# Attention weights turned by VectorE and SBUF-to-SBUF transfers in place of TensorE transposes

## What is computed

```
x: (16, 64, 512)   ctx: (16, 1601, 512)   mask: (64, 1601)   16 heads of 32
q = layernorm(x) @ w_q.T ; k = ctx @ w_k.T ; v = ctx @ w_v.T          (per head)
scores = where(mask == 0, -1e9, q k^T / sqrt(32)) ; attn = softmax(scores)
x = x + (attn v) @ w_o.T
x = x + attention_with_lora(layernorm(x)) ; x = x + experts(layernorm(x))
```

## Time and profile before

| | us |
|---|---|
| time, median of 3 runs | 772.93 (771.41 to 774.77) |
| span of the profiled execution | 772.6 |
| TensorE matmul busy | 708.0 (92%) |
| VectorE busy | 410.2 (53%) |
| ScalarE busy | 360.6 (47%) |
| GpSimd busy | 289.0 (37%) |
| mean granted TensorE clock | 0.960 |
| first value product of batch 0, from the span's start | 59.17 |
| last output product of the cross-attention ends | 471.1 |

### The profile page before, as it was taken

One profiled execution on the slowest core, in us unless ns is written; L12 is line 12 of the kernel. 1 busy time (PEld: TensorE's weight loads), 2 busy tenths in 40 slices (PEclk: granted clock), 3 DMA queues, 4 the chain that ended last, 5 costly groups with the idle time before them and its releaser, 6 DMA issues.

```text
span 772.6 us, 16928 instructions
## 1 busy us (share of the span) xinstructions
PE 708.0 (92%) x6817; PEld 581.6 (75%) x6817; DVE 410.2 (53%) x938; ACT 360.6 (47%) x665; POOL 289.0 (37%) x259
## 2 busy tenths in 40 slices
PE   1999999999999999999999999999999766999970
PEld 0787788778878887888788977887778554788860
DVE  5834434453344424533543345735368348799965
ACT  2425445453545345535454343533455431599950
POOL 0005135513553255225532453432225132788530
PEclk9999999999999999999999999999999985799995
DMA  8401101220021101110110002021001580999818
GB/s 294 149 1 43 45 2 45 98 91 24 29 98 44 44 2 44 44 39 7 44 44 2 3 3 75 1 79 45 3 29 57 188 303 21 330 394 397 333 52 326
DMA packets 30268, 74.77 MB, mean 97 GB/s; under 512 B 4053, under 2 KB 4437, under 8 KB 29155
## 3 DMA queue, kind: packets, MB, share of 16 engines
q1 hardware_dynamic: 25778, 65.16, 23.6%
q0 software_dynamic: 4400, 8.41, 2.9%
HBM read 66.13 MB, written 13.44 MB: 103 GB/s over the span
## 4 chain that ended last, share of the span: by engine, by line
PE 86%; DVE 6%; DMA 3%; ACT 2%; issue 2%; SPq 0%; POOL 0%; DVEq 0%; POOLq 0%; ACTq 0%
PE bank L188 22%; PE bank L190 21%; PE bank L189 20%; PE bank L194 10%; PE bank L345 4%; PE bank L322 3%; DMA raw<-in_wq 2%; DVE x_sb L1611 1%; PE bank L564 1%; DMA wr<-scratch_ys 1%; PE bank L551 1%; PE bank L665 1%; PE bank L580 1%; DVE wh L1084 1%; DVE stats L1340 0%
## 5 line engine op out<-in xcount | busy, mean ns | idle before, releaser
L1637 POOL TENSOR_SCALAR pp<-pp,rl 128x400 f32<-128x400 f32 x128 | 163.8, 1297 | 234.8 <-DVE rl L1162 234.8
L1217 DVE COPY pt<-bank 128x512 f32<-128x512 f32 x64 | 44.3, 692 | 99.4 <-PE bank L194 99.3
L188 PE MATMUL bank<-chi,wk 128*128 128x400 f32 x256 | 93.5, 365 | 0.0
L844 ACT ACTIVATE pp<-pp,acc 128x400 f32<-128x400 f32 x128 | 79.0, 619 | 28.0 <-DVE acc L1250 27.7
L1250 DVE CUSTOM_DVE_ANT_0 pp<-bank,cap 128x400 f32<-128x400 f32 x128 | 66.8, 569 | 46.5 <-PE bank L322 46.5
L190 PE MATMUL bank<-chi,wk 128*128 128x400 f32 x256 | 88.3, 345 | 0.0
L189 PE MATMUL bank<-clo,wk 128*128 128x400 f32 x256 | 88.3, 345 | 0.0
L188 PE MATMUL bank<-wv,chi 128*128 128x512 f32 x200 | 83.5, 417 | 0.0
L189 PE MATMUL bank<-wv,chi 128*128 128x512 f32 x200 | 78.5, 393 | 0.0
L190 PE MATMUL bank<-wv,clo 128*128 128x512 f32 x200 | 78.5, 392 | 0.0
L761 ACT ACTIVATE pt<-bank 128x512 f32<-128x512 f32 x64 | 38.2, 597 | 76.4 <-PE bank L194 75.3
(11 more groups left out here) (238 smaller groups left out, 1387.4 us busy)
## 6 DMA issues: line engine op xcount, KB each, us to landing
wr<-in_We SPq DMA_DIRECT2D x13, 1024.0 KB, 11.6
craw<-in_ctx SPq DMA_DIRECT2D x16, 800.0 KB, 4.4
raw<-in_We SPq DMA_DIRECT2D x8, 1024.0 KB, 10.5
acc<-in_We SPq DMA_DIRECT2D x6, 1024.0 KB, 11.0
scratch_xn<-acc SPq DMA_DIRECT2D x16, 256.0 KB
wr<-scratch_ys SPq DMA_DIRECT2D x8, 512.0 KB, 7.2
x_sb<-in_x SPq DMA_DIRECT2D x2, 1024.0 KB, 8.5
out_dram<-x_sb SPq DMA_DIRECT2D x8, 256.0 KB, 5.9
```

The lines of the kernel that those rows point to most:

```text
L188: pe.matmul(o, lhs[0], rhs[0], start=start, stop=False)
L844: act.activation(frame(p8), frame(p8), ACT.Exp, bias=bias, scale=-1.0, accum_out=total).then_inc(S["a_exp"], 1)
L1217: dve.tensor_copy(pt[:, p8 % 4, :, :].rearrange("p a c -> p (a c)"), at("t", 8 * (n - 1) + p8)[:, :]).then_inc(S["v_pt"], 1)
L1637: pool.tensor_scalar(frame(p8), frame(p8), rl[:, n % 2, p8:p8 + 1], None, ALU.mult).then_inc(S["g_pn"], 1)
```

## The change

- The 32 TensorE transposes of a batch and the 8 copies of their banks go. VectorE now turns each finished frame in blocks of 32x32 (`turn`, one `transpose` of 128x512 per frame) into `square`, which is the space of `raw` read as 16 groups of 256 values per partition.
- SyncE puts the blocks in their place (`shuffle`): for a whole batch 16 transfers from 32 partitions to 32 partitions, in runs of 256 values (1 KB), 128 KB each, from `square` to `pt`. They wait for all eight frames of the batch and for both `pv_part` of the batch before. `pt` is twice as large.
- TensorE's order: keys 0 to 2, first half of the scores, keys 3, the first value tile, both `pv_part` of batch n-1 behind all 16 transfers of it, second half of the scores, the other value tiles. Products of weights and values go to bank 3 (`turned`), so banks 0 to 2 go round.
- VectorE's order: three of the last batch's turnings at the head of a batch, the others behind maxima and shares. ScalarE's exponentials of frames 6 and 7 stand behind the copy of the second value tile.
- `raw` being used, `wo` is loaded and split at batch 0, `w2q` is loaded behind the last transfers, `w2k` behind the barrier to the next stage. `oh` has room for two output tiles, so the third and fourth are filled behind batch 15.

```diff
-        oh = [sb(f"oh{j}", [128, 4, EARLY * 128], f32r, lasting) for j in range(2)]
+        oh = [sb(f"oh{j}", [128, 4, 2 * 128], f32r, lasting) for j in range(2)]
-        pt = sb("pt", [128, 4, 4, 128], f32, second)
+        pt = sb("pt", [128, 4, 4, 256], f32, second)
+        square = raw[:, :].rearrange("p j k n -> p (j k n)").rearrange("p (b x) -> p b x", b=16)
...
+        for n in range(16 * NC_):
+            uses += [("k", 4 * n + g) for g in range(4) if n] + [("v", j) for j in range(made(n), made(n + 1))]
...
         def at(what, i):
-            return pb[use_of[what, i] % 4]
+            return pb[use_of[what, i] % 3]
...
-            def t_part(n, p8):
-                pe.wait_ge(S["g_pn"], 8 * n + p8 + 1)
...
-                turn4(pe, at("t", 8 * n + p8), lambda i4: weight_columns(n, p8, i4)).then_inc(S["p_t"], 1)
             def pv_part(n, half):
-                pe.wait_ge(S["v_pt"], 4 * n + 2 * half + 2)
-                pe.wait_ge(S["a_pt"], 4 * n + 2 * half + 2)
                 if half == 0:
+                    pe.wait_ge(S["d_sh"], 256 * (n + 1))
...
+                for n in range(16 * seg, 16 * seg + NB):
+                    if n:
+                        for g in range(3):
+                            k_part(n, g)
+                    s_part(n, 0)
+                    if n:
+                        k_part(n, 3)
+                    v_part(n, values[0])
+                    if old:
+                        pv_part(n - 1, 0)
+                        pv_part(n - 1, 1)
+                    s_part(n, 1)
+                    for j in values[1:]:
+                        v_part(n, j)
+                for half in range(2):
+                    if not seg:
+                        early_out(2 * half)
+                        early_out(2 * half + 1)
+                    pv_part(last, half)
...
+                    exps(n, seg, 0)
+                    exps(n, seg, 1)
+                    value(n, values[0])
+                    exps(n, seg, 2)
+                    value(n, values[1])
+                    exps(n, seg, 3)
...
+            def turn(n, p8):
+                dve.wait_ge(S["g_pn"], 8 * n + p8 + 1)
+                if n and p8 == 0:
+                    dve.wait_ge(S["d_sh"], 256 * n)
+                c = D * p8 + PW - CW * (n % 8) % 128
+                dve.transpose(square[:, :, 32 * p8:32 * p8 + 32],
+                              pp[:, c:c + 512].rearrange("p (b x) -> p b x", b=16)).then_inc(S["v_pt"], 1)
...
+            def shuffle(n):
+                sp.wait_ge(S["v_pt"], 8 * n + 8)
+                if n:
+                    sp.wait_ge(S["p_pv"], 2 * n)
+                of = square.rearrange("p (i a) x -> p a i x", a=4)
+                for a in range(4):
+                    for to in range(4):
+                        sp.dma_start(pt[32 * to:32 * to + 32, :, a, :],
+                                     of[32 * a:32 * a + 32, to]).then_inc(S["d_sh"], 16)
```

More of the change, by code:

```diff
@@ L229, in perceiver @@
         uses = [("q", m) for m in range(4)] + [("k", g) for g in range(4)] + [("q", 4 + m) for m in range(4)]
[L230 to L241, removed]
+        for n in range(16 * NC_):
+            uses += [("k", 4 * n + g) for g in range(4) if n] + [("v", j) for j in range(made(n), made(n + 1))]
+            if n == NB - 1:
+                uses += [("e", i) for i in range(EARLY)]
         use_of = {use: n for n, use in enumerate(uses)}
         def read_by(what, i):
-            if what == "t":
-                return S["a_pt" if i % 2 else "v_pt"], i // 2 + 1
             if what == "k":
@@ L415, in tensor @@
+                if seg:
+                    spread(last)
             turn_x(0)
@@ L850, in cross @@
-                    value(made(n) + 2)
-                    value(made(n) + 3)
-                    if not seg and 0 <= n - SPLIT < EARLY:
+                    exps(n, seg, 0)
[4 more added lines that the diff above has]
+                    exps(n, seg, 3)
+                    for j in values[2:]:
+                        value(n, j)
+                    if not seg and 0 <= n - SPLIT < 2:
@@ new lines, in cross @@
+                for n in range(first, last + 1):
+                    old = n > first
+                    if old:
+                        for p8 in (5, 6, 7):
+                            turn(n - 1, p8)
+                    if n < last:
+                        context(n + 1)
+                    if n:
+                        k_part(n, 1)
+                    if n == 0:
+                        weight_lo(wh[0], raw[:, 0], 4)
+                    maxima(n, seg, 0)
+                    maxima(n, seg, 1)
+                    share(n, 0, seg)
+                    if n:
+                        k_part(n, 3)
+                    share(n, 1, seg)
+                    turn(n, 0)
+                    turn(n, 1)
@@ L1227, in cross @@
                     if old and seg:
[L1228 removed]
+                        o_more(n - 1, n - 1 - first)
                     elif old:
                         o_first(n - 1)
[L1231 to L1237 removed]
@@ L1261, in cross @@
-                    share(n, 3, seg)
+                    maxima(n, seg, 2)
+                    maxima(n, seg, 3)
+                    share(n, 2, seg)
+                    turn(n, 2)
+                    share(n, 3, seg)
+                    turn(n, 3)
+                    turn(n, 4)
+                    if not seg and 0 <= n - 1 - SPLIT < 2:
+                        dve.wait_ge(S["a_h"], n - SPLIT)
+                        early_lo(n - 1 - SPLIT).then_inc(S["v_h"], 1)
+                for p8 in (5, 6, 7):
+                    turn(last, p8)
@@ new lines, in cross @@
+                if not seg:
+                    for i in range(2):
+                        dve.wait_ge(S["a_h"], i + 3)
+                        early_lo(i + 2).then_inc(S["v_h"], 1)
+                        dve.wait_ge(S["p_o"], i + 1)
+                        early_add(i).then_inc(S["v_x1"], 1)
+                    for i in range(2, EARLY):
+                        dve.wait_ge(S["p_o"], i + 1)
+                        early_add(i).then_inc(S["v_x1"], 1)
+                if seg:
+                    o_more(last, NB - 1)
+                else:
+                    o_first(last)
```

235 lines of the change are left out of this document (87 added, 148 removed).

## The result

The changed kernel takes 781.29 us (median of 5 runs, 777.41 to 783.79), the kernel before on the same chip 772.97 us (771.41 to 775.19): a ratio of 1.0091, 95% interval 1.0057 to 1.0125. It is slower by 0.9%, where 753 us had been forecast. The profiled execution took 777.41 us, its span is 775.6 us, 3.0 above the span before.

The account below looks back on a forecast made before the run. TensorE was taken to bound the batches. Start at 71.6 plus intervals of 347.8 gave 419.4, the end 451.4 in place of 471.1; 19.7 off the 772.6 span, plus 0.3 for the median, gave 753 us, range 728 to 798.

Parts of the forecast that it names:

- What goes: TensorE's transposes, 3.6 us a batch, 58 us in all; intervals would be 21.5 us with three value tiles, 24.4 with four.
- The turnings: VectorE's eight 128x512 transposes a batch, taken at 0.6 us each, 4.8 a batch; the last ends 9.3 behind the second scores.
- rival of longer turnings: VectorE's turnings take twice the length, adding 1.1 us to each of 15 intervals: 770 us, chance 0.05.
- S: Time from first issue to last landing of a batch's 16 transfers, taken as 11.5 us, range 8.5 to 13.2.
- issue-bound: Rival: issuing, not bytes, limits the 16 transfers, 6.2 + 2.3 = 8.5 us to the last landing: 731 us, chance 0.17.
- the circle: Second scores, exponentials, shares, turnings, transfers, `pv_part`, next second scores: 11.5 us plus the transfers' 11.5, 23.0 a batch.
- half-rate rival: Transfers between 32 partitions run at 192 GB/s, 13.2 us to the last landing, intervals of 24.7: 777 us, chance 0.13.
- The clock: TensorE's clock stays up through 1.5 us waits in batches; longer waits at start and end cost 3.3 us each.
- clock rival: TensorE's clock falls at each of thirteen batch waits, 3.3 us each, surely from 2 to 3 us on: 796 us, chance 0.15.
- Start: Splitting `wo` in batch 0 delays second scores from 62.9 to 68.3, a 5.4 us wait, plus 3.3 for the clock: 71.6.
- End: After the last second scores: 20.9 us until transfers land, TensorE waiting 9, then clock 3.3, `pv_part` 2.1, output products 5.7.
- The sum: Start 71.6, fifteen intervals 347.8, then the end to 451.4 in place of 471.1: 19.7 us less, span 752.9.

Follow-up runs that it names:

- e8: Changed kernel with the product of batch n-1 behind second scores and two value tiles, exponentials ahead of value copies, maxima ahead of turnings: 737.4 us, ratio 0.954.
- e4: Changed kernel with eight of each batch's 16 transfers issued by ScalarE and eight by SyncE: 783.8 us, ratio 1.010.
- e11: e10 with all four early output products ahead of the last batch's two products, in place of two ahead and two between: 728.5 us, ratio 0.942.
- e7: Changed kernel with the splitting of `wo` behind the exponentials and maxima of frames 0 to 3 of batch 0: 784.8 us, ratio 1.015.
- e10: e8 with the splitting of `wo` behind the first exponentials and all maxima of batch 0 ahead of VectorE's part: 734.5 us, ratio 0.950.

## Why the prediction was wrong, point by point

- **What goes** was right: 50 us of TensorE's busy time, and in e8, where nothing stands in the way, an interval of 21.98 where 21.5, or 24.4 with four tiles (mean 21.9), had been worked out.
- **The turnings** took 0.69 alone and 0.62 in a row, 0.6 was taken. The last one ended 9.3 behind the scores in nine of the fifteen batches, as forecast, and 9.6 to 10.4 in the others (9.96 in batch 5). The rival of longer turnings fell.
- **S**, the step that failed. It was put at 11.5, the larger of 6.2 for the issues and 9.2 for the bytes, plus 2.3. The issue was wrong: 0.39 us, from four loads of 40 KB into 20 partitions, where it takes 0.64. With 0.64 the same sum gives 16 x 0.64 + 2.3 = 12.5, what batch 5 has; the trace has it as 15 issues of 0.645 and 2.8 from the last issue to its landing. The bytes were less far off: with the issues out of the way and no context to load, e4 took 10.5 to 10.8, forecast 11.5. A nearer row stood in the trace of before, in SyncE's queue, the two loads `qc<-in_rows` of 64 partitions that the prediction had used for its rate of bytes:

```profile
2.13 1.20 SPq L1762 DMA_DIRECT2D qc<-in_rows  x2
```

  That is 0.6 us an issue. So issuing was the limit, as the rival "issue-bound" had it, but through the same 0.39 that rival took it for a gain, S = 8.5, where the true price made the circle longer than the forecast's. That the 777 us of the half-rate rival lie near the measured time is luck: there bytes make S, at 13.2.
- **The circle** as a form was right: 11.5 + S, to within 0.5 in batch 5 (24.48) and to 0.2 in batch 13 (24.0 with S = 12.7). 24.2 in place of the forecast mean of 23.2 makes 14.9 us over fifteen intervals.
- **The clock.** I held that a wait of 1.5 us leaves it. The waits were 2 to 3 us, as the clock rival had named them. Of thirteen such waits (2.0 to 3.1 us) five had a fall with them and eight had none, and the lengths don't part them: 2.0, 2.0, 2.8, 2.9 and 3.1 with a fall, 2.1 to 2.8 without. A fall lasted 3.4 us; the five intervals are 7.3 us over 24.2 together, so a fall cost 1.5, not 3.3. With 2.5 in the first interval this is 10 us more. The rival's price was too high, and its condition, the length of the wait, held in five cases of thirteen.
- **Start.** Second scores at 68.34, forecast 68.3, wait 5.1 for 5.4. The 3.3 put down for the clock there were not to be added to the start: 2.5 of them are in the first interval.
- **End.** From the last second scores to the weights of the next stage 36.8 us, forecast 32.0: the wait for the transfers was 9.6 for 9, but behind the last product came another 4.5, and the weights themselves took 2.1 more at the lower clock. What ends these 4.5 us the profile doesn't name, and the forecast had no term for them. It isn't the load of `w2q`: that was issued at 465.25 and had landed at 470.02, before the last product began. Between the product and the weights the code branches past the further chunks; VectorE takes 2.9 us over this way before and after the change (473.40 to 476.25). That TensorE's 4.5 us are the same is not shown. In e11, with another order, the wait there is for `w2q`, which lands at 427.98, and the weights start at 428.12.
- **The sum.** Against the forecast span: 14.9 + 10.0 in the intervals, -3.3 for the clock counted twice, 4.8 + 2.1 at the end, and -5.3 for the rest of the second stage (-3.1) and the last stage (-2.2), where none was forecast and no run here tells why. That is 23.2; the spans differ by 22.7 (775.6 against 752.9). The median is 28 us over the forecast: 3.9 us more because the profiled run was the fastest of the five, and 1.5 because a run's time lies 1.8 us above its span (777.4 and 775.6), where the forecast took 0.3.

The range of 728 to 798 holds the time; the direction was wrong. The mechanism that decided, the product of the batch before inside the circle, was in the prediction, and its length was off by 1 us in 23. With 1.5 us of waiting forecast in a batch, every further microsecond of S counted in full, and the forecast left no room for it: the gain of 19.7 us in the span became a loss of 3.0.

## What to carry to other kernels

When work moves from TensorE to transfers, ask first how long the way from its inputs to its result is, and then how much other work lies between: here the same slow transfers cost nothing once the product stood one piece later in the program (e8). Count issues as well as bytes, and take the price of each from the row that is nearest in shape; where two limits come out close, lifting one shows little, and only lifting both tells them apart. Ask also what the lifted one lets in: the second queue brought the load of the context forward into the transfers (e4). A wait that is moved out of one place reappears behind it unless what follows has room (e7, e10).

## What was not expected of the hardware

- An issue of a transfer inside SBUF took 0.60 to 0.61 us in the median on SyncE's queue and 0.63 to 0.65 on ScalarE's, with 64 KB or 128 KB, with 64 runs or 128, from 32 partitions or 128.
- The load of the context took 0.33 us to issue before (16 of 16) and 0.59 to 0.60 (13 of 13) when it stood right behind the 16 transfers. Why, no run here tells.
- Transfers between groups of 32 partitions kept the DMA engines busy at 0.81 for 175 GB/s, those over all 128 at 0.54 for 182.
